# Expert tiles of 256 rows with still weights, rounded half an expert at a time beside the tiles

## The reference

```python
x = x + attention(layernorm(x), w_kv_down, w_kv_up, w_q, w_out)   # causal, 16 heads
f = layernorm(x).reshape(4096, 128)
logits = f @ Wr
top_vals, top_idx = top_k(logits, 2)
rw = softmax(top_vals)
g = einsum('nc,ech->neh', f, Wg)                # 128 -> 512, 8 experts
u = einsum('nc,ech->neh', f, Wu)
eo = einsum('neh,ehc->nec', silu(g) * u, Wd) * 12 ** -0.5
x = x + sum over the two chosen experts of rw * eo
```

## Time and profile before

| | us |
|---|---|
| median of 3 timed runs | 909.01 (908.9 to 909.35) |
| the profiled execution's own time | 901.64 |
| its span | 899.6 |

### The profile page before, as it was taken

The page is one execution under the profiler, slowest core; times in us unless marked ns, Lnnn a source line. Parts: engine busy times, 40 slices in busy tenths (PEclk is TensorE's granted clock), DMA queues, the critical chain, the costliest instruction groups (busy, mean ns, idle before and its releaser), DMA issues. The chain is left out here.

```text
span 899.6 us, 20256 instructions
## 1 busy us (share of the span) xinstructions
PE 874.8 (97%) x6153; PEld 643.0 (71%) x6154; DVE 640.3 (71%) x2404; ACT 617.3 (69%) x1614; POOL 589.2 (65%) x598
## 2 busy tenths in 40 slices
PE   7999999999999999999999999999989999999995
PEld 3667667676767766777677767666657888888884
DVE  5677787878778787778777787888885664554542
ACT  4777777777777777777787787767785454445442
POOL 4385476578467748865795677576566677656664
PEclk9999999999999999999999999999999999999998
DMA  6495530000000000000000000000002333333332
GB/s 190 190 350 230 198 90 1 1 25 13 1 11 28 1 2 19 19 2 7 19 13 2 13 26 1 1 19 19 2 19 56 44 58 55 45 47 45 46 47 24
DMA packets 44006, 44.49 MB, mean 49 GB/s; under 512 B 4352, under 2 KB 35968, under 8 KB 43920
## 3 DMA queue, kind: packets, MB, share of 16 engines
q0 software_dynamic: 16528, 26.03, 12.0%
q1 hardware_dynamic: 27392, 17.39, 7.0%
HBM read 15.28 MB, written 28.12 MB: 48 GB/s over the span
## 5 line engine op out<-in xcount | busy, mean ns | idle before, releaser
L376 POOL TENSOR_TENSOR prob<-prob,row_inv 128x512 f32<-128x512 f32 (+3 forms) x256 | 319.3, 1266 | 213.1 <-DVE row_inv L713 213.0
L527 ACT ACTIVATE prob<-prob,neg_max 128x256 f32<-128x256 f32 (+3 forms) x512 | 280.5, 550 | 8.9 <-DVE neg_max L706 2.3
L1140 PE MATMUL low_ps<-PT,v_sb 128*64 128x512 f32 (+3 forms) x1024 | 152.0, 439 | 1.2 <-ACT PT L533 1.2
L1140 PEld LDWEIGHTS low_ps<-PT,v_sb 128*64 128x64 f32 x1024 | 68.1, 136 | 92.8 <-issue 60.4
L718 DVE COPY PT<-low_ps 128x512 f32<-128x512 f32 (+1 forms) x128 | 104.9, 819 | 35.5 <-PE low_ps L1127 33.6
L462 POOL DMA_INDIRECT out<-prob,meta_row x71 | 110.6, 1558 | 27.6 <-issue 26.4
L1127 PEld LDWEIGHTS low_ps<-ident,prob 128*128 128x128 f32 x640 | 74.5, 140 | 55.3 <-POOL prob L376 29.5
L538 ACT ACTIVATE v_sb<-mid_ps 128x512 f32<-128x512 f32 x64 | 38.2, 597 | 102.2 <-PE mid_ps L1070 102.0
L706 DVE CUSTOM_DVE_ANT_0 prob<-mid_ps,mask 128x128 f32<-128x128 f32 (+1 forms) x256 | 93.5, 421 | 5.6 <-PE top_ps L1113 0.2
L996 DVE TENSOR_TENSOR prob<-mid_ps,prob 128x512 f32<-128x512 f32 x71 | 49.1, 691 | 66.3 <-ACT prob L628 58.8
L527 ACT ACTIVATION_READ_ACCUMULATOR prob<-prob,neg_max 128x1 f32 x512 | 95.6, 187 | 0.0
(11 more groups left out here) (203 smaller groups left out, 1775.4 us busy)
## 6 DMA issues: line engine op xcount, KB each, us to landing
routed_rows<-W_dn POOLq DMA_DIRECT2D x8, 2080.0 KB, 7.9
qk_sb<-routed_rows SPq DMA_DIRECT2D x71, 65.0 KB, 1.9
X<-in_L_attn_x SPq DMA_DIRECT2D x8, 256.0 KB, 5.5
W_ffn<-in_L_ffn_Wg SPq DMA_DIRECT2D x8, 256.0 KB, 5.1
W_ffn<-in_L_ffn_Wu SPq DMA_DIRECT2D x8, 256.0 KB, 5.3
W_dn<-in_L_ffn_Wd SPq DMA_DIRECT2D x8, 256.0 KB, 4.5
out<-X SPq DMA_DIRECT2D x8, 256.0 KB, 2.3
out<-prob,meta_row POOLq DMA_INDIRECT x71, 3.3
```

The costliest lines, as they stand in the source:

```text
L376: nc.gpsimd.tensor_tensor(p_pair(i), p_pair(i), row_inv[:, i, :].unsqueeze(2).to_broadcast([P, 2, P * (i + 1)]), ALU.mult).then_inc(S["nor ...
L527: nc.scalar.activation(p_at(i, h), p_at(i, h), ACT.Exp, bias=neg_max[:, i, h:h + 1], scale=-1.0, accum_out=row_sum[:, i, h:h + 1]).then_in ...
L1140: last = nc.tensor.matmul(y_ps[h * HD:(h + 1) * HD, j * P:T], v_sb[:, half, j, o + h * HD:o + (h + 1) * HD], PT[:, h, j, j:NT, :].rearrang ...
```

## The change

- 39 tiles of 256 rows (a pair of slots each) take the place of 71 of 128 rows: 78 slots. A slot is now half of the hidden columns (256 of g and of u) for 256 rows in the products, and 128 rows in the scatter.
- In `tile_up` the weights are the still operand and the 256 transposed rows move: per slot g and u have two pieces of 128 hidden columns each, three products a piece, twelve in all. The hidden values come out transposed, so `tile_hT`, its four transposes and ACT's copy go. The down projection keeps its four float32 products a slot; its sums for a pair gather in one of two buffers, and DVE scales both halves when both slots are done.
- All `split_hi` and `split_lo` go. For each slot ACT rounds half an expert's weights (`unit_hi`, 128 by 512) and DVE subtracts (`unit_lo`), into one of two buffers in `qk_sb`. Both read the slot's expert number from the table into a register.
- Rows come in loads of 256, into four buffers in `X`, which is why SP and the table on DVE wait until six sequences have been stored. The results have eight buffers (`SPOTS`) where four were.
- The scatters keep their rule and their 128 rows. The first 32 slots are early ones. The expert counts are rounded to 256 rows.
- The order at the seam: the first row transposes and unit 0's weights in the last attention step; u of slot 0, the last attention values, g of slot 0, the last output projection.
- The loops over the ring are written out on every engine.

```diff
-SLOTS = (NTOK * K + E * (P - 1)) // P
+PAIR = 2 * P
+ALL = (NTOK * K + E * (PAIR - 1)) // PAIR
+SLOTS = 2 * ALL
-EARLY_TURNS = 7
+EARLY = 32
+SPOTS = 2 * RING
...
+            def unit_hi(j):
+                e = nc.scalar.value_load(table[0:1, 0, bass.ds(j // 2 * 2, 1)], min_val=0, max_val=E - 1)
+                seen(act, S["s_ready"], NT * STEPS)
+                seen(act, S["g_ready"], j - 1)
+                seen(act, S["u_ready"], j - 1)
+                nc.scalar.activation(w_unit[j % 2][:, 0, :, :], ffn_halves[:, bass.ds(e, 1), j % 2, :, :].rearrange("p e b n -> p (e b) n"),
+                                     ACT.Copy).then_inc(S["unit_hi"], 1)
...
+            def turn(j):
+                if j % 2 and j + 1 < SLOTS:
+                    tile_xT(j // 2 + 1)
+                if j + 1 < SLOTS:
+                    unit_hi(j + 1)
+                if j == EARLY - 2:
+                    act.wait_ge(S["table_done"], 2)
+                tile_silu(j)
...
+            def unit_lo(j):
+                e = nc.vector.value_load(table[0:1, 0, bass.ds(j // 2 * 2, 1)], min_val=0, max_val=E - 1)
+                seen(dve, S["unit_hi"], j + 1)
+                nc.vector.tensor_tensor(w_unit[j % 2][:, 1, :, :], ffn_halves[:, bass.ds(e, 1), j % 2, :, :].rearrange("p e b n -> p (e b) n"),
+                                        w_unit[j % 2][:, 0, :, :].bitcast(F32), ALU.subtract).then_inc(S["unit_lo"], 1)
...
+            def turn(j):
+                if j % 2 and j + 1 < SLOTS:
+                    tile_xT(j // 2 + 1)
+                if 1 < j + 1 < SLOTS:
+                    unit_lo(j + 1)
+                if j < SLOTS:
+                    tile_h(j)
+                if j % 2 == 0:
+                    if j:
+                        tile_eo(j // 2 - 1)
+                    if j < SLOTS:
+                        tile_meta(j // 2)
...
+            def tile_up(j, dst, part):
+                for c in range(2):
+                    last = passes(dst[:, c * PAIR:(c + 1) * PAIR],
+                                  [w_unit[j % 2][:, a, part, c * P:(c + 1) * P] for a in range(2)],
+                                  [xT_tile[j // 2 % 2][:, a, :] for a in range(2)], True, True)
+                return last
...
+            def turn(j):
+                ahead = j % 2 and j + 1 < SLOTS
+                if ahead:
+                    tile_xT(j // 2 + 1)
+                if j < SLOTS:
+                    tile_g(j)
+                    tile_u(j)
+                if ahead:
+                    load_expert(j // 2 + 1)
+                tile_down(j - 1, expert(j - 1))
...
+            def scatter_slot(j):
+                q, spot = j % RING, j % SPOTS
+                last = S[f"eo_out{(j - 1) % RING}"]
+                seen(pool, S[f"eo_out{(j - 2) % RING}"], landings(j - 2))
+                if j >= RING:
+                    pool.wait_ge(last, nc.gpsimd.value_load(table[0:1, 2, bass.ds(j, 1)], min_val=16, max_val=16 * (SLOTS // RING + 1)))
+                elif j == 2:
+                    pool.wait_ge(last, 16)
+                seen(pool, S["eo_done"], j + 1)
```

More of the change, by code:

```diff
@@ L53, in seen, with slots_of, landings @@
         eng.wait_ge(sem, count)
[L56 to L62, removed]
+def slots_of(t):
+    return range(2 * t, 2 * t + 2)
+def landings(j):
+    return 16 * (j // RING + 1) if j >= 0 else 0
 def layer(nc, x, w_down, w_up, w_q, w_out, Wr, Wg, Wu, Wd, out):
@@ L478, in _ @@
             pool.wait_ge(S["x_out"], 16 * COUNTED)
[L479 to L482, removed]
+            for j in range(EARLY):
+                scatter_slot(j)
+                late(j)
             pool.wait_ge(S["table_done"], 2)
             pool.wait_ge(S["x_late"], 16 * (B - COUNTED))
[L485 to L489, removed]
+            for j in range(EARLY, SLOTS):
+                scatter_slot(j)
         @block.scalar
@@ L636, in turn @@
-            def turn(m, q, first=False, last=False, drain=False):
-                if not last and not drain:
-                    tile_xT(*after(m, q))
-                if not first:
-                    tile_hT(*before(m, q))
-                if not drain:
-                    tile_silu(m, q)
-            def late(j):
-                if j == 5:
-                    post_xn2T(B - 1)
-            tile_xT(0, 0)
-            post_out(B - 1)
-            for m in range(EARLY_TURNS):
-                for q in range(RING):
-                    turn(m, q, first=(m == 0 and q == 0))
-                    late(RING * m + q)
@@ L655, in _ @@
-            with act.Fori(EARLY_TURNS, TURNS) as m:
-                for q in range(RING):
-                    turn(m, q)
-            for q in range(LEFT):
-                turn(TURNS, q, last=(q == LEFT - 1))
-            turn(TURNS, LEFT, drain=True)
+            for j in range(SLOTS):
+                turn(j)
+                late(j)
         @block.vector
@@ L735, in step @@
                     inv(n, 2)
-                for e in SPLIT_LO.get(n, []):
-                    split_lo(e)
                 if pre is not None and k == 1:
@@ L1006, in turn @@
-            def turn(m, q, first=False, last=False, drain=False):
-                if not last and not drain:
-                    tile_xT(*after(m, q))
-                if not drain:
-                    tile_h(m, q)
-                if not first:
-                    tile_eo(*before(m, q))
-                if not drain:
-                    tile_meta(m, q)
+                seen(dve, S["down_ready"], j - 1)
+                nc.vector.tensor_tensor(h_sb[j % 2], u_ps[j % 2], silu_sb[j % 2], ALU.mult).then_inc(S["h_done"], 1)
@@ L1032, in late @@
                     table_late(j - 12)
-            tile_xT(0, 0)
-            for m in range(EARLY_TURNS):
-                for q in range(RING):
-                    turn(m, q, first=(m == 0 and q == 0))
-                    late(RING * m + q)
-            with dve.Fori(EARLY_TURNS, TURNS) as m:
-                for q in range(RING):
-                    turn(m, q)
-            for q in range(LEFT):
-                turn(TURNS, q, last=(q == LEFT - 1))
-            turn(TURNS, LEFT, drain=True)
+            for k in range(1, NP):
+                step(NP * (B - 1) + k, k, nxt=k < NP - 1, post=B - 2)
+            unit_lo(1)
+            for j in range(SLOTS + 1):
+                turn(j)
+                late(j)
         @block.tensor
```

317 lines of the change are left out of this document (131 added, 186 removed).

## The result

The changed kernel takes 928.35 us (median of 4; 926.5 to 929.65) beside 908.95 us for the kernel before on the same chip: a ratio of 1.021, with an interval of 1.020 to 1.023. Forecast were 921.7 us and a range of 906 to 936. The sign and the mechanism held. The size is short by 6.7 us: the start and the chain of scatters were mis-sized in the sum, and PE's slot in the working beside it.

The account below looks back on a forecast made before the run. POOL's chain of expert scatters, each waiting for an earlier landing, was taken to set the end, with PE also close to its limit. Median 909.01 + 5.3 for a later last scatter + 7.4 for subtractions holding POOL = 921.7 us, range 906 to 936.

Parts of the forecast that it names:

- the start: End of attention: fewer weight subtractions before the first product let the first scatters start 1.3 us earlier, between 0 and 3.
- PE's slot: PE in the expert stage: 1.40 + 0.89 + 0.52/5 = 2.39 us a slot, against 2.88 a tile before.
- POOL's chain sets the end: Expert scatters waiting for landings carry the sum: slot 77 starts at 897.4, 5.3 us later than its like before.
- The subtraction: VectorE's two-SBUF-input subtraction before every slot holds POOL: 0.2 us for each of 37 links, 7.4 us, bounds 0 and 22.
- The step that gave 9.01 for a run of three: POOL's chain, slots 28 to 43 before: 45.07/5 = 9.01 us; one more scatter, 1.94, makes 10.95 a run of four.
- The 0.117 a product: PE's up projections: each 256-column product with its weight load takes 0.117 us, near the lower row 0.111; twelve take 1.40.
- PE's gain: PE alone in the expert stage: 192.3 us against 210.4, 18.1 less.
- The rival at 890: Scatters keep up and PE decides the end: 18.1 us less from PE and about 1 at the start; chance 0.06.
- VectorE's 2.25 under PE's slot: VectorE in the expert stage: 1.57 us a tile plus 0.68 for the low half, 2.25, hidden under 2.39.
- the rival at 945: Weight preparation on ScalarE and VectorE decides: 3.1 us a slot, 37 more than 210.4, about 945; chance 0.08.
- The median as the base: Differences are added to the timed median, 909.01 us, not to the profiled execution's 901.64.
- six signs: Expert stage: PE share below 97%, its and VectorE's waits, scatter distances 1.94 and 2.8, scatters over 1.6, early PE end, 1.40 products.

Follow-up runs that it names:

- the one-source operation: Changed kernel with VectorE's subtraction of weights replaced by an operation of the same size with one SBUF input: 923.17 us, against 928.35.
- the second profile: The kernel before, unchanged, profiled once more: 907.75 us, span 905.8.
- the two runs on the start: Changed kernel with ScalarE's rounding of unit 1 ahead of the last attention copy: 927.87 us; or with POOL's normalisation behind the second scatter: 926.95 us.
- two small moves: Changed kernel, scatters waiting for the landing three before, plus POOL's normalisation behind the second scatter and its small power behind the sixth: 904.18 us, ratio 0.995.

## Why the prediction came out as it did

- **POOL's chain sets the end: right, shown.** The same scatters without their wait for j-2 inside an expert give back 20 us, without existing at all 27.6; in the kernel before nothing and 6.3. The forecast starts against the measured ones, from slot 1 on: to slot 2 4.3 against 4.25; 2 to 6 10.7 against 12.0; 6 to 12 16.1 against 16.1; 12 to 24 37.9 against 40.4; 24 to 56 87.6 against 92.5; 56 to 66 25.6 against 26.0; 66 to 77 26.3 against 26.3. That is 208.5 against 217.5.
- **The subtraction: right in kind, its size not measured by itself.** The forecast had 7.4 on top of the 208.5; the chain shows 9.0 in this profile. The runs give 4.1 for one added to the kernel before and 5.2 for the second source taken away, and both also change how long VectorE's queue is. That 7.4 and 9.0 lie close is in part luck, since some of the 9.0 is not from the subtraction: the distance behind scatter 43 is 5.74 us (823.69 to 829.43), and 5.45 with the one-source operation. POOL's gate there waits until 828.72, 5.0 after the scatter's start, where the earlier trace rows has landings of 3.2 to 3.8. Why that landing is late was not tried. The step that gave 9.01 for a run of three took it from the stretch behind the one long distance in before (scatters 27 to 28, 4.71 us), and so priced no such landing.
- **PE's slot: mis-sized, 2.39 forecast, 2.55 measured.** The 0.117 a product was right (0.12), though its reason, near the lower of two rows, was a choice. The sum left out the 0.10 that the first product of a slot adds and the pause of 0.13 ahead of it in every other slot; transposes came out at 0.13 a pair. The tile before was 2.93, not 2.88. PE's gain was 9.1 us and not 18.1, before the first twenty slots took 4.6 of it. None of this entered the forecast, in which POOL's chain carries the sum. The rival at 890, in which PE decides, was thereby never to be had: without any scatter the changed kernel takes 900.8.
- **VectorE's 2.25 under PE's slot: right in the steady part, wrong at the start.** Without scatters PE is busy for 100 of 100 us from 750 to 850, so nothing of the preparation shows there, and the rival at 945 falls. In the first twenty slots the last sequence's work on the same queue makes PE wait, which "with little to spare" named and the sum put at 0. There PE waits for weights that VectorE has not subtracted yet, 5.2 us in all without scatters.
- **The start: wrong in sign, -1.3 forecast, +2.2 measured.** I moved the first scatter with the first product. But with two halves of an expert's weights for 256 rows the first output needs two slots of PE, and both of its scalings come together (VectorE L988 x2 at 690.67) after the down products of slot 1; before, one tile was enough (688.99, in the second profile). That is 1.7 at the first scatter (690.29, 691.95); the way to the second, with the normalisation in it, takes 7.09 where it took 6.59. By these distances it is 3.5 of the 6.7 us by which the forecast was short, if the chain hands the start on to the end, which the two runs on the start do not show; the chain from the second scatter on gives 2.1, the end of the span 0.5, and 0.6 lies between profiles and medians.
- **The median as the base: right.** Adding differences of one profile to the median was needed: the profile of before was 7.4 us under its median, 5.8 of it in the attention stage by the second profile, and its own 901.64 plus the sum would have missed by 14.
- **What would show it.** Of the six signs five came: PE's share in the stage (91%), its waits for VectorE and VectorE's for a landing, distances of 1.94 and 2.8 in turn with some of 2.3, scatters over 1.6 us, and PE's end with six scatters still to start. The sixth, 1.40 for twelve products, was 1.53.

## What to carry to other kernels

An engine that is busy for 65% of the time can set the end if its work is a chain of waits for landings: read the distances between its starts, not its share, before pricing a change that gives the busiest engine less to do. When such a chain is found, first ask whether each wait in it is needed; here one landing less in the rule was worth 20 us in the changed kernel, which brought a loss of 2% to nothing, and with two small moves it became a gain of 0.5%. A coarser tile changes what the first output needs, so work out the first output by itself.

## What the runs showed of the hardware

- A one-column operation of POOL (gate) takes 0.18 us alone, 0.72 behind a scatter, and 1.12 where a VectorE subtraction of two SBUF tensors of 0.69 us meets it. One such subtraction a tile, added to the kernel before, costs POOL 0.12 us a tile on average (60 ns in the scatter, 64 in the gate).
- PE's 256-column products with a weight load each stand 0.12 us apart, the 512-column ones of the kernel before 0.23, and the first of a slot adds 0.10.
- A scatter-accumulate of 128 rows of 128 lands 3.3 us after its start as a rule; a few take 4 to 5, as that of scatter 43 in the changed kernel (5.0) and without the second source (4.7).
- Two executions of the same kernel differed by 5.8 us at the end of the attention, with the same instructions, in steps of 0.6 to 0.9 and one of 2.1.
